# A float32 transformer layer on one core: the K products of both first units made ahead, from two x buffers

## The reference

```python
Q = split_heads(x, 16)                 # the queries are x itself
K = split_heads(x @ Wk + bk, 16)       # 256 columns, 16 per head
V = split_heads(x @ Wv + bv, 16)       # 1024 columns, 64 per head
attn = softmax(Q K^T + causal mask)
o = (attn @ V), heads joined
x1 = layernorm(x + (x + gelu(o) @ Wf + bf))
h = silu(x1 @ wg^T) * (x1 @ wu^T)      # int weights times 1/127, hidden 768
out = layernorm(x1 + h @ wd^T)
```

## Time and profile before

| | |
|---|---|
| median of 3 runs | 1959.52 us (1958.96 to 1960.97) |
| the profiled execution, its own time | 1962.14 us |
| its span | 1960.4 us |
| PE busy | 1855.1 us (95%) |
| DVE, ACT, POOL busy | 1424.2, 1039.1, 1158.1 us |
| first score tile on PE | 47.77 us |
| first scoreT on PE (step 2) | 85.38 us |
| granted TensorE clock, mean | 0.976 |

### The profile page before, as it was taken

The page is one execution under the profiler, slowest core; times in us unless marked ns, Lnnn a source line. Parts: engine busy times, 40 slices in busy tenths (PEclk is TensorE's granted clock), DMA queues, the critical chain, the costliest instruction groups (busy, mean ns, idle before and its releaser), DMA issues. The chain is left out here.

```text
span 1960.4 us, 38648 instructions
## 1 busy us (share of the span) xinstructions
PE 1855.1 (95%) x10304; PEld 961.9 (49%) x10304; DVE 1424.2 (73%) x3469; ACT 1039.1 (53%) x1523; POOL 1158.1 (59%) x1328
## 2 busy tenths in 40 slices
PE   6799999999999999999999999989898999999996
PEld 5344444444444444444444444333255777767773
DVE  3877877777786777778677777767537787887874
ACT  2155555555555555555555556555554564555643
POOL 2187777777768777776877786887832122221222
PEclk9699999999999999999999999999899999999998
DMA  8955556455565545555454664456157667566610
GB/s 267 252 152 158 166 138 185 132 175 158 143 181 132 173 132 174 159 144 182 132 170 131 178 166 142 116 156 151 60 133 181 182 158 190 167 160 180 163 55 22
DMA packets 261008, 303.55 MB, mean 155 GB/s; under 512 B 28048, under 2 KB 177680, under 8 KB 260880
## 3 DMA queue, kind: packets, MB, share of 16 engines
q1 hardware_dynamic: 260880, 302.19, 55.6%
HBM read 174.20 MB, written 127.93 MB: 154 GB/s over the span
## 5 line engine op out<-in xcount | busy, mean ns | idle before, releaser
L964 ACT ACTIVATE weights<-ring 128x1024 f32<-128x1024 f32 (+3 forms) x768 | 599.2, 810 | 332.8 <-PE ring L704 328.1
L672 POOL TENSOR_TENSOR weight_sum<-weight_sum,weights 128x512 f32<-128x512 f32 (+3 forms) x448 | 682.0, 1522 | 9.8
L704 PE MATMUL o_acc<-weights,v_pair 128*64 128x512 f32 (+3 forms) x3072 | 620.1, 510 | 10.8 <-POOL weights L636 6.0
L1109 DVE TENSOR_REDUCE part_max<-ring 128x2 f32<-128x1024 f32 x256 | 301.3, 1218 | 129.4 <-PE ring L704 129.4
L636 POOL TENSOR_SCALAR_AFFINE_SELECT weights<-weights 128x256 f32<-128x256 f32 x512 | 217.6, 430 | 298.1 <-ACT weights L964 297.4
L695 POOL TENSOR_TENSOR h_lo<-hidden,h_hi 128x512 f16<-128x512 f32 x96 | 114.2, 1191 | 391.2 <-ACT h_hi L933 391.2
L704 PE MATMUL ring<-q_stack,k_stack 50*128 50x512 f32 (+3 forms) x1536 | 308.4, 407 | 37.6 <-DVE rowmax L1117 23.0
L1117 DVE CUSTOM_DVE_ANT_0 scrap<-ring,causal 128x128 bf16<-128x128 f32 (+3 forms) x512 | 229.5, 486 | 135.4 <-PE ring L704 132.0
L704 PE MATMUL ring<-k_stack,q_stack 48*128 48x512 f32 (+3 forms) x1536 | 304.2, 399 | 18.0 <-DMA k_stack<-k_rows 8.9
L704 PEld LDWEIGHTS o_acc<-weights,v_pair 128*64 128x64 f32 x3072 | 174.4, 137 | 234.1 <-issue 198.8
L1117 DVE CUSTOM_DVE_ANT_0 scrap<-ring,causal,part_max 128x128 bf16<-128x128 f32 (+3 forms) x512 | 251.1, 546 | 47.6 <-PE ring L704 47.2
(11 more groups left out here) (105 smaller groups left out, 2057.5 us busy)
## 6 DMA issues: line engine op xcount, KB each, us to landing
v_pairs<-v_unit SPq DMA_DIRECT2D x64, 512.0 KB, 3.5
v_pair<-v_pairs SPq DMA_DIRECT2D x64, 512.0 KB, 5.3
o_heads<-o_pair SPq DMA_DIRECT2D x64, 512.0 KB, 3.5
g<-o_heads SPq DMA_DIRECT2D x16, 2048.0 KB, 8.1
den_wide<-reciprocals SPq DMA_DIRECT2D x32, 1024.0 KB, 13.3
q_stack<-q_rows SPq DMA_DIRECT2D x128, 192.0 KB, 3.7
k_stack<-k_rows SPq DMA_DIRECT2D x128, 192.0 KB, 4.3
q_rows<-x_hi SPq DMA_DIRECT2D x32, 512.0 KB, 3.6
```

What stands on the lines that cost most here:

```text
L672: pool.tensor_tensor(dst, other, W[t][:, :, :], ALU.add).then_inc(s_add, 1)
L704: return nc.tensor.matmul(o, l, r, start=start, stop=stop)
L964: nc.scalar.activation(W[t][:, :, :], bank_of("t", t)[:, :, 0:width_of(t)], ACT.Exp).then_inc(s_w, 1)
L1109: v.tensor_reduce(part[r % 2][:, u - 4, :], bank_of("s", j)[:, :, 0:w], AX.X, ALU.max).then_inc(s_max, 1)
```

## The change

- **Two x buffers.** The x of units 0 and 1 are both loaded at the start (`xt`, and a new `xt_early`), and split into `x_hi`, `x_lo` and into `x_early_hi`, `x_early_lo`. K of unit 1 is split into `k_early_hi`, `k_early_lo`. These buffers lie where `wi_in` and the attention's weights lie later.
- **K first.** PE makes the two K jobs of unit 0 and those of unit 1 behind each other, into the four halves of ring banks 0 and 1. DVE's order is: split x of unit 0, Wk, x of unit 1, then the four K tiles.
- **Wv is split elsewhere.** ACT copies Wv to `wv_hi`, POOL subtracts to make `wv_lo`, ahead of its eight memsets, which now wait for it.
- **V of unit 0** (8 jobs) follows on PE before the first score, through four banks. **V of unit 1** goes into step 0: one job per burst, into `oo[1]`.
- **SP's order.** q rows of both units, k rows of both, stacks of pair 0, x of unit 2, V tiles of unit 0, Wf and the feed-forward weights; then in step 0 stacks of pair 1, q rows of unit 2, V tiles 0 to 2 of unit 1; in step 1 stacks of pair 2, V tile 3 of unit 1, V of pair 0 (before in step 0), V of pair 1, the shifts. 
- The feed-forward weights are cast by DVE at the end of step 1 instead of step 0, and ACT waits for them, and for the stored rows, at step 2.

```diff
+        xt_e = sb("xt_early", [P, DC, U], F32, lctx)
+        ke_hi = sb("k_early_hi", [P, DC, U], F32R, lctx)
+        ke_lo = sb("k_early_lo", [P, DC, U], F32R, lctx)
+        xe_hi = sb("x_early_hi", [P, DC, U], F32R, lctx)
+        xe_lo = sb("x_early_lo", [P, DC, U], F32R, lctx)
         lctx.close()
...
-        a_banks = [rg[0][:, 0], rg[0][:, 1], rg[1][:, 0], rg[1][:, 1], rg[2][:, 0]]
+        k_banks = [rg[0][:, 0], rg[0][:, 1], rg[1][:, 0], rg[1][:, 1]]
+        v_banks = [rg[2][:, 0], rg[2][:, 1], oo[0][:], oo[1][:]]
...
+            def store_early_v(a, i):
+                sp.wait_ge(s_eev, NV * a + 2 * (i + 1))
+                put_v(a, i)
...
-                if r < PAIRS:
+                if r == 1:
+                    store_early_v(1, UT - 1)
+                    load_v(0, 0)
+                if 1 <= r < PAIRS:
                     load_v(r, it)
                 if 1 <= r <= PAIRS:
                     move_shifts(n - 1)
...
                 if a is not None and k == 0:
                     store_q(a)
+                if r == 0:
+                    for i in range(UT - 1):
+                        store_early_v(1, i)
...
-            load_x(0, True)
+            load_early_x(0)
             sp.dma_start(wk_in[:], Wk.rearrange("(c p) n -> p c n", p=P)).then_inc(s_wk_in, 16)
+            load_early_x(1)
             sp.dma_start(wv_in[:], Wv.rearrange("(c p) n -> p c n", p=P)).then_inc(s_wv_in, 16)
...
-            for a in range(ALONE):
-                store_q(a)
-                load_x(a + 1)
-                store_k(a)
-                if a == 1:
-
-                    sp.wait_ge(s_krows, 2 * RING)
-                    load_stacks(0, 0)
-                for i in range(UT):
-                    store_v(a, i)
+            store_early(0)
+            store_early(1)
+            store_early_k(0)
+            store_early_k(1)
+            sp.wait_ge(s_krows, 2 * RING)
+            load_stacks(0, 0)
+            load_x(ALONE, True)
+            for i in range(UT):
+                store_early_v(0, i)
...
+            pool.wait_ge(s_wvhi, 1)
+            pool.tensor_tensor(wv_lo[:], wv_in[:], wv_hi[:].bitcast(F32), ALU.subtract).then_inc(s_wvs, 1)
             pool.wait_ge(s_const, 4)
+            pool.wait_ge(s_wvs, 1)
             for i in range(RING):
...
+            pe.wait_ge(s_wks, 1)
             for a in range(ALONE):
-                pe.wait_ge(s_xs, a + 1)
-                for j in range(NJ):
...
+                pe.wait_ge(s_xes, a + 1)
+                for j in range(DC):
+                    job(j, k_banks[DC * a + j], *((x_hi, x_lo), (xe_hi, xe_lo))[a], s_ej)
+            pe.wait_ge(s_wvs, 1)
+            for v in range(NV):
+                if v >= NVB:
+
+                    pe.wait_ge(s_eev, v - NVB + 1)
+                job(DC + v, v_banks[v % NVB], x_hi, x_lo, s_ej)
+
+            pe.wait_ge(s_eks, DC * ALONE)
+            pe.wait_ge(s_eev, NV)
...
+                    if r == 0:
+
+                        if b >= 1:
+                            pe.wait_ge(s_eev, NV + b)
+                        job(DC + b, oo[1][:], xe_hi, xe_lo, s_ej)
                     job_beside(r, it, b)
...
+            act.wait_ge(s_wv_in, 16)
+            copy(wv_hi[:], wv_in[:]).then_inc(s_wvhi, 1)
...
-                    if b == 7 and r == 0:
+                    if b == 7 and r == 1:
                         ffn_weights()
```

More of the change, by code:

```diff
@@ L223, in build @@
         s_w_hi = sem("weights_hi_ready")
-        s_wkv = sem("wkv_split")
+        s_wks = sem("wk_split")
+        s_wvhi = sem("wv_hi_ready")
+        s_wvs = sem("wv_split")
+        s_xe = [sem(f"early_x_loaded{i}") for i in range(2)]
+        s_xeh = sem("early_x_hi_ready")
+        s_xes = sem("early_x_split")
+        s_ej = sem("early_projection_ready")
+        s_ekh = sem("early_k_hi_ready")
+        s_eks = sem("early_k_split")
+        s_eev = sem("early_v_copied")
         s_wrest = sem("ffn_weights_ready")
@@ L361, in _, with load_early_x, store_early, store_early_k @@
         def _(sp):
-            def load_x(a, first=False):
-                if not first:
-                    sp.wait_ge(s_xs, a)
-                    settle(sp, s_passed["sp"])
+            def load_early_x(a):
+                sp.dma_start((xt, xt_e)[a][:], xT[a // 2:a // 2 + 1, :, a % 2 * U:a % 2 * U + U].rearrange(
+                    "o (c p) t -> (o p) c t", p=P)).then_inc(s_xe[a], 16)
+            def store_early(a):
+                hi, lo = ((x_hi, x_lo), (xe_hi, xe_lo))[a]
+                sp.wait_ge(s_xes, a + 1)
+                store_rows(qd, (hi, hi, lo), s_qst, a)
+            def store_early_k(a):
+                hi, lo = ((k_hi, k_lo), (ke_hi, ke_lo))[a]
+                sp.wait_ge(s_eks, DC * (a + 1))
+                store_rows(kd, (hi, lo, hi), s_kst, a)
+            def store_early_v(a, i):
+                sp.wait_ge(s_eev, NV * a + 2 * (i + 1))
+                put_v(a, i)
+            def load_x(a, first=False):
+                if first:
+                    sp.wait_ge(s_xes, 1)
+                else:
+                    sp.wait_ge(s_xs, a - ALONE)
+                settle(sp, s_passed["sp"])
                 sp.dma_start(xt[:], xT[bass.ds(a // 2, 1), :, bass.ds(a % 2 * U, U)].rearrange(
@@ L704, in mm, with job @@
                 return nc.tensor.matmul(o, l, r, start=start, stop=stop)
-            def job(j, a, bank, chunks=range(DC)):
+            def job(j, bank, x_hi, x_lo, ready):
                 what, i, hf = JOBS[j]
                 last = 3 * DC - 1
-                for c in chunks:
+                for c in range(DC):
                     if what == "k":
@@ L935, in _, with copy_v, copy_early_v @@
             act.preload_act_table_set(LN_EXP)
-            def copy_v(j, a, bank, first=False):
+            def copy_v(j, a, bank):
                 what, i, hf = JOBS[j]
-                act.wait_ge(s_job, NJ * a + j + 1)
-                if not first and hf == 0:
+                act.wait_ge(s_job, NJ * (a - ALONE) + j + 1)
+                if hf == 0:
                     act.wait_ge(s_vst[i], 16 * a)
                 copy(vs[:, i, BANK * hf:BANK * (hf + 1)], bank).then_inc(s_ev, 1)
-            for a in range(ALONE):
-                for j in range(DC, NJ):
-                    copy_v(j, a, a_banks[(NJ * a + j) % NB], a == 0)
-            act.wait_ge(s_wkv, 2)
+            def copy_early_v(a, v, bank):
+                what, i, hf = JOBS[DC + v]
+                act.wait_ge(s_ej, DC * ALONE + NV * a + v + 1)
+                if a and hf == 0:
+                    act.wait_ge(s_vst[i], 16 * a)
+                copy(vs[:, i, BANK * hf:BANK * (hf + 1)], bank).then_inc(s_eev, 1)
+            act.wait_ge(s_wv_in, 16)
+            copy(wv_hi[:], wv_in[:]).then_inc(s_wvhi, 1)
+            for v in range(NV):
+                copy_early_v(0, v, v_banks[v % NVB])
+            act.wait_ge(s_wks, 1)
+            act.wait_ge(s_wvs, 1)
             act.wait_ge(s_const, 4)
-            act.wait_ge(s_wrest, 3)
             def exponent(t, rt, n):
@@ L1096, in _ @@
                 for c in range(DC):
[L1097 to L1102 removed]
+                    split_early_k(a, c)
             def top(j, r, n):
```

110 lines of the change are left out of this document (63 added, 47 removed).

## The result

The changed kernel takes **1948.66 us** (median of 5 runs, 1947.72 to 1952.17), the kernel before, run beside it, 1959.54 (5 runs, 1958.96 to 1961.72): a ratio of 0.9946, with 95% between 0.9931 and 0.996. The profiled execution took 1948.38 us with a span of 1946.7.

The account below looks back on a forecast made before the run. PE is full in the loop, so its start, set by the DMA queue to the shifts, counts: scoreT 2.3 us earlier, minus 1.7 for a cold start, is -0.6, from 1959.52 to 1958.9 us; range 1953.0 to 1963.7.

Parts of the forecast that it names:

- So what this chain can gain is holes, not bytes: DMA queue up to pair 0's shift load: same 21.9 MB in both kernels, so scoreT only 2.3 us earlier.
- 2.62 MB at 330 GB/s are 7.9 us: Ahead of the first score: V of unit 0 and x of unit 2 leave the queue, saving 7.9 us.
- The second half of the same step: Queue from pair 1's scores (58.9 us) to the shift load's issue (81.4), with both V loads at 205 GB/s, 5.1 us.
- Rival A: Queue runs faster: last part at 330 instead of 298 GB/s, 3.1 us less, 1955.8; at full length 1950.5; chance 0.28.
- Everything after it is the same work in both kernels: Behind the first scoreT: PE is full and the work unchanged, so no difference expected in the loop behind 100 us.
- The cold start: First scoreT: PE idle from 76.4 to 83.1 us then runs at a lower clock, a price of 1.7 us (ends 0 and 2.5).
- issue of the shift load to scoreT: Between the shift load's issue (81.4 us) and scoreT (83.1): 1.4 plus 0.3 us, with 1.0 and 4.4 as bounds.
- Step 0 with its eight V jobs: PE in step 0: 16.6 us plus eight V jobs, partly in gaps, makes about 22.6 us, ending at 59.3.
- rival B: Step 0 stays cold: V jobs take 20.6 us at 0.43 us apart, step 1 ends at 91.0, 1965.1 us; chance 0.07.
- GpSimd: Start: Wv subtraction in two times 2.38 us, then eight memsets, done at 28.5 us; stacks may go at 30.2.
- rival C: GpSimd holds the stacks: DVE's k splits shut it out for 6 us, stacks 4.3 us later, 1963.2 us; chance 0.05.
- Rival D: Start: K is not ahead because x of unit 1 lands late; next to no chance.

Follow-up runs that it names:

- vmid: Changed kernel, with only SP's order altered: V tiles of unit 0 back between the K rows of unit 0 and the rows of unit 1; 1961.83 us, ratio 1.0027.
- vlate: Changed kernel with the V loads of pairs 0 and 1 moved behind the shift stores and shift load of pair 0; 1947.28 us, ratio 0.9943.

## Why the prediction was wrong

The forecast was 1958.9 us, a gain of 0.6; it is 10.9.

- **"So what this chain can gain is holes, not bytes"** is the step that failed. It took the same bytes at the same rates (330, 298, 205 GB/s) and left only pauses to gain. But the 330 was an average over kinds. Of the 22 us of the earlier trace rows, 7.26 MB, the V and x taken out are 2.62; the other 4.64 at 407 GB/s take 11.4 us, 10.6 less, where "2.62 MB at 330 GB/s are 7.9 us" stood. Measured: the stacks are issued 14.1 us earlier, 3.2 of them the hole, so 10.9. Two things make up the missing 2.7 us, by an estimate from the stretches. The V tiles were the slow part: at their own 283 GB/s 2.10 MB are 7.4 us, not 6.4. And what is left of the 22 us, rows and x together, moved 353 GB/s, where the rows by themselves move 407. That small pauses hidden by the share did this isn't shown: before, the engines were at work nearly as much with the V tiles as with the rows (0.96 and 1.04), and in vmid, where they really wait for a tile, the share falls to 0.61. The pace of the tiles has a part in their rate (283 GB/s one by one, 347 with four ready), but even these stay below the rows. First score 33.43 instead of 36.7.
- **The second half of the same step.** From pair 1's scores to the shift load I had 22.5 us (58.9 to 81.4), measured are 19.25. The V loads ran at 297 GB/s between 72 and 75 us, not at 205: 1.05 MB are 3.5 us instead of 5.1. The stretch of the earlier trace rows from 75 to 79 us was misread. It isn't a V load alone; the last stacks of pair 2, issued at 68.08, landed at 78.7 in it, and the V of pair 1 at 80.1. So the transfers do not strictly follow each other: a V load beside stacks moved 205 GB/s together, two V loads by themselves 297. Where the other 1.6 us lie isn't shown; from 56 to 68 us the changed kernel moved 298 GB/s, like before. The hole came as said. Over the whole chain the engines worked 5.0 us less on the same bytes, by the means of three profiles, and the forecast had nothing there; why the same packets cost less in the new order stays open beyond these two places.
- **Rival A** had the direction ("rates differ by kind in the stretches" was the argument for it, and right; "the kinds and their bytes are the same" was the one against it, true but not enough, since the order was different), with 3.1 us in one part, and 9 at full length, "for which no row speaks". Its chance was in the 0.28, but the range ended at 1953.0.
- **"Everything after it is the same work in both kernels"** failed as an accounting. The work is the same, but not its phases: 2.75 us up to pair 48, of which 1.6 are blocked casts (253.0 to 251.4) and 1.1 the second steps (the 2.75 as a whole is not clear of the scatter; the second steps are, 220.3 against 219.2 in all three). A sign of it was to be had before: the cast's mean of 1.27 us against the 0.69 of the earlier trace rows.
- **The cold start** was right in kind: PE idle for 5.09 us (6.7 forecast), the clock at 0.50 up to about 85 us. As a price against before it was 2.1 us in the first pair of profiles (31.50 from scoreT to row sums against 29.39), but before has 32.04 and 30.72 in its other two: a cold start there too. By the means 0.8, not 1.7. The start of scoreT at 85.38 with the full clock was one case of several.
- **Right:** issue of the shift load to scoreT, 1.93, 1.97 and 1.93 us (1.7 taken, between 1.0 and 4.4). The Trainium skill ("DMA: Bandwidth & Descriptors", Anatomy of one DMA) has 2.0 us for one DMA, from GpSimd's queue; with the same 0.3 us for the second issue that gave 2.3, further off than the 1.7. Step 0 with its eight V jobs, 22.3 us (22.6). So rival B fell: it began at less than the full clock (0.76 from 33 to 40 us) and had 1.00 from 40 to 47.
- **GpSimd** was quicker than said: `wv_lo` 4.56 us from 13.34 (forecast 2 x 2.38), the eight memsets 7.99 us from 18.02, so done at 26.0, not 28.5. The stacks go 1.2 us later, when the rows have landed, and not on GpSimd's word: rival C fell, and there was no block here: `wv_lo` ran beside the K splits and took less than forecast. In the loop a block by GpSimd does matter, where I had not looked.
- **Rival D** fell: all three row stores of unit 1's x are issued by 13.44 us.

What stays open: the second and fourth kinds of step, why the phases of the changed order spare the cast, why the same packets took less of the DMA engines' time, and whether vlate's order is worth its 1 us. It is the fastest measured, but can't be told from the changed kernel.

## What to carry to other kernels

A DMA share near 1 is no rate: price what is moved or taken out by the GB/s of its own kind, from a stretch that holds nothing else, before concluding that only holes can be gained, and ask for each store in an in-order queue whether its data is ready or is being made. Put the stores that others wait for ahead of those whose data comes in step with a slower engine; moving the work on the engines without moving the queue brought nothing here. Differences of a few microseconds behind the change need more than one profile of each kernel.

## What the runs showed of the hardware

- Row stores in 2 KB packets moved 407 GB/s back to back, at a share of 1.05 (393 at 1.04 before). V tiles in 512 B packets moved 283 at 0.96 when they came one by one, and 347 at a share of 1.14 to 1.15 when four lay ready.
- Stacks and a V load side by side moved 205 GB/s at a share of 1.02, two V loads by themselves 297 at 1.10.
- A cast of 128x1024 float32 on DVE takes 0.69 us, and up to 1.8 when GpSimd's addition has begun just before it. A step became longer by 0.3 to 0.7 us, in the loop, only where the cast took more than 1.6; casts of up to 1.49 did no harm, nor did those of 1.54 to 1.71 at pairs 0, 4, 8 and 48.
- The granted clock falls to half within the attention loop's last steps, with PE's gaps there of 0.2 to 0.7 us, and costs such a step 1.6 us; how many steps differs from execution to execution.
- The start of one and the same kernel varies by up to 4 us between executions (shift load at 72.91 to 76.28), against a gain of 7.8 at the row sums.
